# Late normalisations of the last batch in a transformer layer: in consecutive units of one pair of head groups, or spread over three pairs with the low halves on GpSimd

## What is computed

```python
xq = rms_norm(x @ wq.T) * q_norm_w        # 32 heads of 64
xk = rms_norm(x @ wk.T) * k_norm_w        # 8 heads of 64, each used by 4 query heads
xv = x @ wv.T
scores = xq @ xk.T / 8 + alibi            # causal, window of 256
out = softmax(scores) @ xv
x = x + layernorm(out @ wo.T)
```

## Time and profile before

| | us |
|---|---|
| median of 3 runs | 1378.05 (1374.04 to 1379.8) |
| the profiled execution | 1375.0 |
| its span, first to last instruction | 1373.2 |
| busy in the span: PE, DVE, ACT, POOL | 1246.4, 956.3, 768.3, 362.4 |
| pair 0 of the attention, 317.27 to 372.60 | 55.33 |
| pair 1, 372.60 to 404.44 | 31.84 |
| pair 3, 436.04 to 467.67 | 31.63 |
| pair 4, 467.67 to 500.40 | 32.73 |

### The profile page before, as it was taken

The page is one execution under the profiler, slowest core; times in us unless marked ns, Lnnn a source line. Parts: engine busy times, 40 slices in busy tenths (PEclk is TensorE's granted clock), DMA queues, the critical chain, the costliest instruction groups (busy, mean ns, idle before and its releaser), DMA issues.

```text
span 1373.2 us, 30808 instructions
## 1 busy us (share of the span) xinstructions
PE 1246.4 (91%) x9148; PEld 1049.4 (76%) x9148; DVE 956.3 (70%) x2514; ACT 768.3 (56%) x2013; POOL 362.4 (26%) x443
## 2 busy tenths in 40 slices
PE   5999999985899989999999999999799998989894
PEld 4778787864777778888888888888677786868683
DVE  4587777758899978888888888888544655362623
ACT  3555454635799977877777877778222321222221
POOL 1000000010377763443444434434211001020201
PEclk9999999996799999999999999999899999999997
DMA  4226262556455553544544444433433322020100
GB/s 154 96 98 228 108 258 97 216 202 238 155 179 178 174 192 119 172 125 137 171 127 151 137 131 164 152 125 120 146 113 112 107 92 93 1 84 9 47 15 32
DMA packets 94445, 180.38 MB, mean 131 GB/s; under 512 B 7456, under 2 KB 36256, under 8 KB 94368
## 3 DMA queue, kind: packets, MB, share of 16 engines
q1 hardware_dynamic: 94368, 179.42, 38.1%
HBM read 107.83 MB, written 71.57 MB: 131 GB/s over the span
## 4 chain that ended last, share of the span: by engine, by line
PE 56%; issue 24%; DVE 10%; DMA 4%; ACT 3%; POOL 2%; DVEq 1%; SPq 0%; POOLq 0%; ACTq 0%
PE bank L1133 17%; PE bank L1201 13%; PE bank L1155 7%; PE bank L1164 7%; PE bank L1263 4%; PE bank L1190 2%; DVE pT_lo L951 2%; DVE u_sb L944 2%; PE bank L1180 2%; PE bank L1182 2%; PE bank L1181 2%; DVE inv_rms L898 1%; DMA wo_stage<-woT 1%; DMA o_in<-o_scr 1%; ACT p_sb L747 1%
## 5 line engine op out<-in xcount | busy, mean ns | idle before, releaser
L747 ACT ACTIVATE p_sb<-u_sb,low 128x384 f32<-128x384 f32 (+2 forms) x512 | 274.2, 535 | 82.1 <-DVE low L944 54.9
L944 DVE CUSTOM_DVE_ANT_0 u_sb<-bank,bias 128x384 f32<-128x384 f32 (+2 forms) x512 | 231.8, 453 | 64.5 <-PE bank L1155 45.2
L1164 PE MATMUL bank<-ident,p_sb 128*128 128x128 f32 x1152 | 224.5, 286 | 43.4 <-DVE pT_lo L951 39.2
L1155 PE MATMUL bank<-k_st,q_st 128*128 128x384 f32 (+2 forms) x1024 | 253.9, 330 | 5.6 <-DVE v_out L918 2.9
L951 DVE TENSOR_TENSOR pT_lo<-bank,pT_hi 128x384 f16<-128x384 f32 (+2 forms) x512 | 232.0, 453 | 26.9 <-ACT pT_hi L755 16.4
L755 ACT ACTIVATE pT_hi<-bank 128x384 f16<-128x384 f32 (+2 forms) x512 | 205.1, 401 | 51.9 <-PE bank L1164 48.0
L1164 PEld LDWEIGHTS bank<-ident,p_sb 128*128 128x128 f32 x1152 | 140.8, 143 | 83.4 <-ACT p_sb L747 33.0
L1155 PEld LDWEIGHTS bank<-k_st,q_st 128*128 128x128 f32 x1024 | 179.7, 196 | 29.4 <-DVE low L944 3.5
L1263 PE MATMUL bank<-zT_hi,gu 128*128 128x512 f32 x440 | 161.5, 399 | 2.5 <-issue 1.3
L1180 PE MATMUL bank<-v_st,pT_hi 128*128 128x64 f16 x1152 | 157.8, 195 | 0.5 <-DVE pT_lo L951 0.5
L1182 PE MATMUL bank<-v_st,pT_lo 128*128 128x64 f16 x1152 | 157.6, 195 | 0.0
(11 more groups left out here) (109 smaller groups left out, 2469.5 us busy)
## 6 DMA issues: line engine op xcount, KB each, us to landing
q_scr<-qk SPq DMA_DIRECT2D x64, 512.0 KB, 2.7
q_st<-q_scr SPq DMA_DIRECT2D x32, 1024.0 KB, 7.7
k_st<-k_scr SPq DMA_DIRECT2D x64, 256.0 KB, 3.0
o_scr<-o_out SPq DMA_DIRECT2D x128, 128.0 KB, 2.5
o_in<-o_scr SPq DMA_DIRECT2D x16, 1024.0 KB, 5.3
k_scr<-qk SPq DMA_DIRECT2D x16, 512.0 KB, 2.6
x_in<-x SPq DMA_DIRECT2D x4, 1024.0 KB, 8.4
w_stage<-wqT SPq DMA_DIRECT2D x4, 1024.0 KB, 6.3
```

The lines of the kernel that those rows point to most:

```text
L747: nc.scalar.activation(p_sb[:, u % RING, 0:w], u_sb[:, u % RING, 0:w], ACT.Exp, scale=-1.0, bias=low[:, u % RING:u % RING + 1], accum_out= ...
L944: nc.vector.tensor_tensor_reduce(out=u_sb[:, u % RING, 0:w], in0=bank[u % 2][:, 0:w], in1=bias[:, 2 * u // UNITS, u % REP, at:at + w], sca ...
L1155: mm = nc.tensor.matmul(bank[u % 2][:, 0:w], q_st[:, s, r, P * i:P * i + P], k_st[:, s, part, P * key:P * key + w], start=(part == 0), sto ...
L1164: mm = nc.tensor.transpose(bank[2 + u % 2][:, P * j:P * j + P], p_sb[:, u % RING, P * j:P * j + P], ident[:])
```

## The change

The 14 late chunks of the last batch get places in three pairs: in pairs 0, 1 and 2, the units 2, 4, 6, 18 and 20 (in pair 2 without the unit 20). VectorE scales a chunk in that unit (`scale_raw`), ScalarE rounds it one unit later, and GpSimd makes its low part (`split_late`): the chunks of units 2, 4 and 6 behind the bias of the pair's second group, those of 18 and 20 behind the bias of the next pair's first group. SyncE's stores follow: the first three of a pair stand in its queue ahead of `load_wo`. For that, the pairs 0 to 4 are written out on each engine, in place of a loop over pairs 1 to 4. Chunk 5, the last early one, is still split on VectorE, in unit 0 of pair 0.

The diff, cut to its core: the places, the loops, then SyncE, GpSimd and VectorE.

```diff
+LATE_UNITS = (2, 4, 6, 18, 20)
+LATE_NORMS = {}
+for _k, _f in enumerate(range(LATE, QC + KVC)):
+    LATE_NORMS[_k // len(LATE_UNITS), LATE_UNITS[_k % len(LATE_UNITS)]] = _f
...
 def attention_loops(eng, attend):
-    attend(0)
-    with eng.Fori(1, LAG) as n:
+    for n in range(LAG):
         attend(n)
...
             def attend(n, tile=None, wo=False):
                 load_heads(n, 0)
                 store_o(n - 1, 0, [TT - 1])
+                if isinstance(n, int):
+                    store_late(n - 1, UNITS // 2, UNITS)
...
                 store_o(n - 1, 1, [TT - 1])
+                if isinstance(n, int):
+                    store_late(n, 0, UNITS // 2)
                 if wo:
                     load_wo(n - 1)
...
+            def split_late(n, first, end):
+                for f in late_norms(n, first, end):
+                    pool.wait_ge(qk_hi_ready, (QC + KVC) * (B - 1) + f + 1)
+                    pool.wait_ge(qk_ready, (QC + KVC) * (B - 1) + f)
+                    nc.gpsimd.tensor_tensor(out=qk[:, f % QK_RING, 1], in0=raw[:, f], in1=qk[:, f % QK_RING, 0].bitcast(F32),
+                                            op=ALU.subtract).then_inc(qk_ready, 1)
...
                 make_bias(n, q, 1)
+                split_late(n, 0, UNITS // 2)
...
                 make_bias(n + 1, q + 1, 0)
+                split_late(n, UNITS // 2, UNITS)
...
             def attend(n, tile=None):
                 for u in range(UNITS):
                     unit_work(n, u)
-                    if isinstance(n, int) and n == 0 and u + LATE < QC + KVC:
-                        norm(B - 1, u + LATE)
+                    if isinstance(n, int) and n == 0 and u == 0:
+                        split_raw(B - 1, LATE - 1)
+                    for f in late_norms(n, u, u + 1):
+                        scale_raw(B - 1, f)
```

More of the change, by code:

```diff
@@ L95, with late_norms @@
 PIECES = feed_forward_pieces()
+LATE_UNITS = (2, 4, 6, 18, 20)
+LATE_NORMS = {}
+for _k, _f in enumerate(range(LATE, QC + KVC)):
+    LATE_NORMS[_k // len(LATE_UNITS), LATE_UNITS[_k % len(LATE_UNITS)]] = _f
+def late_norms(n, first, end):
+    return [LATE_NORMS[n, u] for u in LATE_UNITS if isinstance(n, int) and first <= u < end and (n, u) in LATE_NORMS]
 def attention_loops(eng, attend):
-    attend(0)
-    with eng.Fori(1, LAG) as n:
+    for n in range(LAG):
         attend(n)
@@ L404, in load_wo, with store_late @@
                              .rearrange("a p c d -> p (a c) d")).then_inc(wo_loaded, DMA)
+            def store_late(n, first, end):
+                for f in late_norms(n, first, end):
+                    store_qk(B - 1, f)
+                    if f == QC + KVC - 1:
+                        stage1_stored(B)
             def attend(n, tile=None, wo=False):
@@ L429, in _ @@
             sp.dma_start(v_norm[:, G:G + 2].rearrange("p g d -> p (g d)"), vn_scr[:, 0:2 * HD]).then_inc(vn_loaded, DMA)
-            for f in range(LATE, QC + KVC):
-                store_qk(B - 1, f)
-            stage1_stored(B)
+            store_late(0, 0, UNITS // 2)
             store_o(0, 0, range(TT - 1))
-            with sp.Fori(1, LAG) as n:
+            for n in range(1, LAG):
                 attend(n, wo=True)
@@ L602, in _ @@
             make_bias(0, 0, 1)
+            split_late(0, 0, UNITS // 2)
             pool.wait_ge(vn_loaded, 2 * DMA)
@@ L606, in _ @@
             make_bias(1, 1, 0)
+            split_late(0, UNITS // 2, UNITS)
             for i in range(TT // 2):
                 finish_o(0, 0, 1, i)
-            with pool.Fori(1, LAG) as n:
+            for n in range(1, LAG):
                 attend(n, n, wo=True)
@@ L770, in attend @@
                     unit_work(n, u)
-                    if isinstance(n, int) and n == 0 and u + LATE < QC + KVC:
-                        norm(B - 1, u + LATE)
+                    if isinstance(n, int) and n == 0 and u == 0:
+                        round_raw(B - 1, LATE - 1)
+                    for f in late_norms(n, u - 1, u):
+                        round_raw(B - 1, f)
                     m, at = divmod(u - START - 1, STEP)
@@ L876, in split_raw, with scale_raw @@
                 nc.vector.tensor_tensor(qk[:, f % QK_RING, 1], raw[:, f], qk[:, f % QK_RING, 0].bitcast(F32), ALU.subtract).then_inc(qk_ready, 1)
-            def norm(b, f):
+            def scale_raw(b, f):
                 dve.wait_ge(inv_ready, 2 * b + f // QC + 1)
@@ L882, in norm @@
                                                ALU.mult, ALU.mult).then_inc(scaled, 1)
+            def norm(b, f):
+                scale_raw(b, f)
                 if f:
```

## The result

| | before | after |
|---|---|---|
| median | 1378.17 (1374.04 to 1379.8, 4 runs) | 1367.83 (1365.38 to 1368.2, 4 runs) |
| the profiled execution | 1375.0 | 1367.75 |
| its span | 1373.2 | 1365.9 |

The ratio is 0.9935, with a 95% interval of 0.9913 to 0.9957: 0.65% or 9 us faster, 5.9 to 12.0 by the interval (the two medians lie 10.3 us apart).

The account below looks back on a forecast made before the run. No engine had much room: VectorE and ScalarE were nearly full, GpSimd 0.1 to 0.3 us to spare after `wo`. Pair 0 -17.5, pairs 1 and 2 +13.1, written-out pairs -1.2: -5.6 us, 1372.5 against the median 1378.05, range 1363 to 1381.

Parts of the forecast that it names:

- The chain through `wo`: Pairs 1 and 2: late splits delay stores, `wo`, GpSimd's casts and VectorE's inversions; 7.4 and 5.7 us longer, together 13.1.
- the 7.4 us: Pair 1: lengthening from fifth `o_mid` ending at 34.9 against 27.55 wanted; VectorE's five scalings fall into that wait.
- Rival C: Pairs 1 and 2: load of `wo` stays slow at 9.0 us, twice 2.8 us more, 1378 us; chance 0.15.
- (c): Pair 0: five scalings on VectorE of 0.66 us each, +3.3 us.
- (a): Pair 0: its first unit keeps the split of chunk 5 and the filling of the pipeline, +0.5 us.
- (b): Pair 0: starts at the lower clock level for five to seven light units, some filling given back, +1.0 us.
- (d): Pair 0: GpSimd's late splits hold back the scalings of units 4 and 6 on the shared port, +1.4 us.
- The seams: Written-out pairs: 0.1 us for each pair's seam and most of pair 4's 1.1 us saved, -1.2 together.
- Rival D: Written-out pairs: loop jumps stall engines, so seams give 1 us each, -9.2 in all, 1368.9 us; chance 0.07.
- A: Pairs 1 and 2: GpSimd has the room, only nine scalings cost, 5.9 us; -12.8 in all, 1365.2 us; chance 0.20.
- B: Pair 0: TensorE's clock stays at the lower level throughout, +13.9, so +8.3 in all, 1386.4 us; chance 0.08.
- No change: Whole kernel: a difference within about 0.5%, 6.9 us; chance 0.52, against 0.38 for faster and 0.10 for slower.

Follow-up runs that it names:

- Experiment 1: The changed kernel with SyncE issuing the load of `wo` ahead of the pair's three late stores instead of behind them: 1359.72 us, ratio 0.9854.
- experiment 4: The changed kernel with three late chunks in each of pairs 1 to 3, GpSimd's splits in two gaps, `wo` loaded ahead of late stores: 1356.64 us, ratio 0.9847.
- Experiment 2: The changed kernel with the late low halves back on VectorE, two units behind their scaling; places and written-out pairs kept: 1382.75 us, ratio 1.0027.
- experiment 3: The kernel before with pairs 1 to 4 written out and the late chunks left in the first pair: 1373.6 us, ratio 0.9967.
- second profile of before: The kernel before, run once more unchanged: 1376.61 us.

## Why the prediction was right, and where it was off

**The chain through `wo` (pairs 1 and 2): right, and this is where the time goes.** Forecast and measured in pair 1, in pair time: bias ends 10.7 and 9.8; splits done 14.8 and 13.9; `wo` issued 15.3 and 14.4; its load 6.2 and 6.5; cast 21.5 and 20.9; fifth `o_mid` done 34.9 and 34.9; pair "about 39" and 39.1. The inversions of units 20 and 28 wait as forecast; in pair 2 only unit 20's does. Experiment 1 is the proof: with `wo` loaded earlier and everything else as it is, 8 us come back. It shows too that the 7.4 us were no sum of independent costs, as the prediction said: 3.4 of the scalings, 1.1 of unit 12 and the 0.6 left over hide in the same wait, and remain once it is gone. Unit 12's wait I had not seen: the chain was followed only from the arrival of `wo` on, and the first `o_mid` behind the three splits was not held against its inversion.

**Pair 2: too low by 1.0 to 1.7 us (37.5 against 39.2 and 38.5).** The mis-sized term is the load, 6.2 taken for both pairs, with 9.0 as an end. In pair 1 the last load of the heads was issued 9.6 us before `wo` (356.44, 366.07), in pair 2 only 7.7 us before it (397.30, 404.98), and there the load took 8.9. Rival C was thus half true. Behind the longer wait the clock fell, which no step had counted.

**Pair 0: 34.5 where 37.8 was forecast, below even my lower bound of 35.4.** Against pair 4 of the same trace, 31.14, units 0 to 7 take 1.5 us more, units 8 to 17 0.2 and units 18 to 31 1.7: 3.4 together, 5 x 0.68. In sum that is term (c), 3.3. (a), 0.5 for filling, and (b), 1.0 for the clock, came to nothing together: unit 0 lasted 1.99 us against 1.25, with VectorE waiting 1.08 us for the rounding of chunk 5, but units 1 to 7, with three scalings in them, only 0.8 more than in pair 4. The pair has 321 matmuls where others have 355, and VectorE never waited for TensorE in it, though the clock was at the lower level at first. The clock is back within 7.3 us of the pair's start (forecast: within 8), as these windows have it:

```profile
317.00:324.50 7.50, 6.00 (x34) 5.10 (x34) 6.13 (x25) 5.72 (x21) 2.00 (x2) 0.58 0.94 306
```

```profile
324.50:351.00 26.50, 24.10 (x276) 19.05 (x276) 24.28 (x88) 23.97 (x78) 15.73 (x17) 1.00 0.57 207
```

In experiment 4 it was at the lower level longer, 0.87 over pair 0 against 0.91, and the pair took 34.58 us against 34.53. (d), 1.4 for the port, failed on the order of the two: the scaling of unit 4 began before the late split that was to hold it back, and GpSimd waited; the next late split began at 324.09, as the scaling of unit 6 (323.42, 0.75 us) ended.

```profile
321.59 0.72 DVE L913 SCALAR_TENSOR_TENSOR raw<-raw,norm_w,inv_rms 128x512 f32<-128x512 f32 x1
...
321.85 1.59 POOL L598 TENSOR_TENSOR qk<-raw,qk 128x512 fp32r<-128x512 f32 x1 [20.25 <-ACT qk L715]
```

The late split took 1.59 us in place of 1.28, and the expected scaling of over 1 us isn't there. And 0.5 us come from the base: a written-out pair is 31.1, not 31.6.

**The port shared by VectorE and GpSimd.** The longest scalings of pairs 0 to 2 lasted 0.89 to 0.96 us in place of 0.75. Each of the five had begun 0.3 to 0.4 us into an `o_out` of 0.73 on GpSimd, and three of them (336.70, 353.87 and 376.30) with no bias near. The scaling at 357.92 has both:

```profile
357.60 0.73 POOL L579 TENSOR_TENSOR o_out<-o_mid,v_norm 128x256 f32<-128x256 f32 x1 [0.20 <-DVE low L980]
...
357.92 0.96 DVE L913 SCALAR_TENSOR_TENSOR raw<-raw,norm_w,inv_rms 128x512 f32<-128x512 f32 x1
```

It is held back by the `o_out`, and then the bias, begun at 358.29 behind it, takes 3.19 us in place of 2.75: there GpSimd waits. The exclusive lock ("SBUF — State Buffer", the section on the two separate sides, in the Trainium skill) asks who starts first; I had applied it with the other order. An event of this kind cost VectorE 0.2 us where I had taken 0.7 for a late split. Experiment 2 has the order that I feared: a subtraction begun 1.18 us into the bias took 2.11 us in place of 0.69. In each of these cases the trace agrees with the rule on who waits; the waits are some 0.1 to 0.2 us shorter than what was left of the other engine's instruction.

**The seams: -1.2 forecast, -3.0 measured,** by experiment 3 (0.7, 0.5, 0.2 and 1.6 us in pairs 1 to 4; -3.7 against the second profile of before). The term took most of pair 4's 1.1 us for a seam, which it isn't, and too little for the others: units 0 and 16 alone give some 0.3 us a pair. In the changed kernel pairs 3 and 4 together came out at 64.5 and 63.7 us against 64.4 and 64.5 of before, since what the seams give, pair 3 loses to its own `wo`: issued at pair time 6.7, before its place in the earlier trace rows, it took 11.0 us to the cast (436.74 to 447.73), right behind the loads of the heads; in experiment 1 the pair is 30.99. Rival D, which took 1 us a seam, was nearer in size than I put it, at 0.3 to 0.7 us in pairs 1 to 3. No run shows what the time in units 0 and 16 of the loop is made of.

**The sum.** -17.5 became -20.8, +13.1 became +14.9, and pairs 3 and 4, forecast at -1.2, gave +0.1: -5.8 in pairs 0 to 4 of the first profile and -7.7 between the second ones, where -5.6 was forecast. Part of the agreement is luck, pair 0's 3.3 us too many against the others' 3.1 too few. And the whole gain was 9 us where 5.6 was forecast. The rest of the 9 us is the 2 to 3 us of the feed-forward, which no reading of the trace of before would have given. The bounds were also added wrongly: those of pair 0, the load and the seams give -10.6 to +3.6, or 1367 to 1382, and not 1365 to 1380; the measured median lies at that lower end.

**The rivals.** A fell: the inversions wait, and pairs 1 and 2 cost 15 us and not 5.9; experiment 4 shows that it was true of GpSimd's room and false of its places. B fell with the clock's early return. No change was given a higher chance than faster: the forecast lay 0.4% below the median, inside the bound, and the 2 to 3 us of the feed-forward alone put the result outside it (-5.6 and those are -7.6 to -8.6, against 6.9).

## What to carry to other kernels

When work is moved to an engine with idle time, ask what stands behind it in every queue: here each late split was cheap, and the load of `wo`, which has nothing to do with it, stood behind its store. Put transfers that somebody waits for ahead of transfers that wait for somebody. And spread the moved work over several gaps of its engine, not behind one long instruction: five splits in bunches of three and two cost a pair 5 us with `wo` early, 1.0 for each, three splits in bunches of one and two 2.0, 0.67 for each, which is only what VectorE paid for its scalings. (Experiment 4 changes the number and the places at once; which of the two counts for more was not tested.)

## What the runs showed of the hardware beside that

- A wait costs more than its length when TensorE starves in it: after five microseconds with 2.70 us of matmuls (411 to 416) the granted clock was 0.50 for the next five and 0.87 over the five behind them, and from unit 21 on pair 2 took 1.4 us more than pair 4. In experiment 1, where no wait for `wo` is left in pairs 1 and 2, it is 1.00 over pairs 1 to 3. But a lower clock cost nothing in pair 0, where VectorE waited only for ScalarE (0.91 or 0.87, 34.53 or 34.58 us).
- A store of 128 KB issued behind 1.6 MB of loads on the same queue released its waiter 4.7 to 7.3 us after the end of its issue (nine profiles), and after 2.6 us when it was issued ahead of them (one). In the first profile of before that is 493.13 to 500.03. The length of pair 5 goes with it: 41.9 us at 4.7, 47.1 at 7.3.
- Taking four passes of a loop apart gave 0.2 to 0.7 us for three passes of 31.6 and 1.6 for the fourth (one profile of each), of which only the 0.3 us of units 0 and 16 came again in every profile. It also changed gaps in which TensorE waited for nothing that the profile shows, some 700 us later, by some 2 us in all, the same way in each of seven profiles.
